# Degrees from run ends, divided loads, layer norm first, and rows of two groups gathered inside the block of degrees

## The chip, the cores and the metric

The kernel runs on one core of one Trainium2 chip. A core has TensorE (PE, matmuls into PSUM), VectorE (DVE), ScalarE (ACT), GpSimd (POOL, which also issues indirect DMAs) and SyncE (SP, which here only issues DMAs and waits), with 16 DMA engines. The metric is the device time of one execution in microseconds; lower is better.

## The reference

A graph of 12,500 nodes with 32 features and 200,000 edges, sorted by target (`dst`); each edge has 16 attributes. Two layers are computed:

```
h = relu(layernorm(x))
m = relu(concat(h[src], edge_attr) @ w1a + b1a) @ w1b + b1b      # per edge
agg = segment_sum(m, dst) / max(count of dst, 1)
x = x + relu(concat(h, agg) @ w2a + b2a) @ w2b + b2b
h = relu(layernorm(x)); f = h
10 times:  f = 0.9 * in_deg^-0.5 * segment_sum((f * out_deg^-0.5)[src], dst) + 0.1 * h
result = x + f
```

`in_deg` and `out_deg` are the numbers of edges that enter and leave a node, at least 1. Everything is float32.

## The kernel before, in words

Nodes stand as 128 partitions by J = 98 columns (node n at partition n mod 128, column n div 128). Edges stand as 128 partitions by T = 1568 columns, in the order of the input, so each partition holds a stretch of edges sorted by target; 704 padding edges fill the last partition. The work is a row of blocks. At the end of a block all engines wait for each other, SP's own waits on DMAs included. `fast_way` calls them in this order:

1. `setup`: SP loads x, the two ends of the edges and the weights, one DMA after another, and waits for all (`loaded`). Each of `src` and `dst` is one DMA of 127 partitions and one of the last, short row. SP then starts a DRAM-to-DRAM copy of all edge attributes (12.5 MB) and doesn't wait for it. VectorE waits for `loaded` and splits each end into partition and column.
2. `degrees(…, 1)`: in-degrees as a matrix product over all edges. For each of 98 groups of G = 16 edge columns, VectorE makes 16 one-hot rows of the partition (L298, 128x2048) and of the column (L298, 128x1568), and PE adds 16 products into one PSUM bank (L329).
3. `layer_norm_relu` on VectorE with one square root of ScalarE, then `store_table`: SP stores h to DRAM as the table of rows (L262) and waits for it.
4. `prepare_sorted`: VectorE works out, in single steps, marks of equal neighbours, keys of edges, and from the in-degrees the first and last edge of each node (L713 to L759). SP stores the keys.
5. `messages_and_counts`: a loop over 98 groups of 16 edge columns, two slots (s = 0, 1) in one pass of the loop. For a group GpSimd issues 16 indirect DMAs (L858), each of which gathers one row of the table for 128 edges, and one fetch of keys for two groups (L839); SP loads the group's attributes into the same rows tile (L884) and stores the counts (L871) and the running sums (L876). PE turns the rows (L1100), multiplies them with the weights (L1117), and counts pairs of source and target by one-hot products (L1083, L1089); ScalarE copies what PE turned (L1028), applies ReLU (L1032) and reads the counts (L1023); VectorE makes the one-hot rows (L963, L967) and adds the sums of runs (L928). GpSimd starts group g when PE has turned group g - 2, whose slot it takes, and VectorE has copied the indices of g (L939), which it does at the start of its own group g - 1.
6. `nodes_of_runs`, a second layer norm, `propagate` (the ten steps, from about 3,900 us on), `needs_general`, `store_result`.

`needs_general` makes a flag; if it isn't zero, `general_way` computes everything anew in a form that needs no sorted edges. It is not run on the reference's data.

Of the kernel before, what the change touches and what calls it, by code (L numbers as in the profile page):

```python
# [6 lines left out]
FP32 = mybir.dt.float32  # L7
BF16 = mybir.dt.bfloat16
FP16 = mybir.dt.float16
# [118 lines left out]

def setup(nc, b, edges, ins):

    with ExitStack() as ctx:
# [7 lines left out]
        LOADS = 17  # L139

        @block.sync
        def _(sp):
# [4 lines left out]
            for tile, ends in ((edges.src[:, 0:T], ins["src"]), (edges.dst, ins["dst"])):  # L147
                sp.dma_start(tile[0:P - 1, :], ends[0:(P - 1) * T].rearrange("(p t) -> p t", t=T)).then_inc(loaded, 16)
                sp.dma_start(tile[P - 1:P, 0:EL], ends[(P - 1) * T:E].rearrange("(p t) -> p t", p=1)).then_inc(loaded, 16)
# [116 lines left out]
def degrees(nc, b, edges, sides):  # L266
# [3 lines left out]
    with ExitStack() as ctx:  # L270
# [47 lines left out]
        def _(pe):  # L318
# [15 lines left out]
            last.then_inc(summed, 1)  # L334

# [314 lines left out]
def prepare_sorted(nc, b, edges, ins, kept):  # L650


    same, cont, last_row, window_row, unsorted = kept
    with ExitStack() as ctx:
# [49 lines left out]
        def _(dve):  # L704
# [20 lines left out]
            step(nc.vector.tensor_reduce(unsorted[:, 0:1], drop[:, :], AX.X, ALU.max))  # L725

# [20 lines left out]
            step(nc.vector.tensor_tensor(start[:, :], start[:, :], b.banks[:, 0, 0:J], ALU.add))  # L747
            nc.vector.tensor_copy(column[:, :], start[:, :]).then_inc(counted, 1)

            step(nc.vector.tensor_tensor(last[:, :], start[:, :], b.in_deg[:, :], ALU.add))  # L750
            step(nc.vector.tensor_scalar(last[:, :], last[:, :], -1.0, 0.0, ALU.add, ALU.max))
            step(nc.vector.tensor_scalar(part[:, :], last[:, :], 1.0 / T, 0.5 / T - 0.5, ALU.mult, ALU.add))
# [22 lines left out]
def messages_and_counts(nc, b, edges, same, window_row, tail, counted_edges, crowded):  # L775
# [8 lines left out]
    with ExitStack() as ctx:  # L784
        sem = lambda name: ctx.enter_context(nc.semaphore(f"{name}_{b.tag}"))
        sb = lambda name, shape, dt=FP32: ctx.enter_context(nc.sbuf_tensor(f"{name}_{b.tag}", shape, dt))
        gathered = [sem(f"gathered{s}") for s in range(SLOTS)]
# [13 lines left out]
        rows = sb("rows", [P, SLOTS, G, 64])  # L801
# [28 lines left out]
        def _(pool):  # L830
# [14 lines left out]
            with pool.Fori(0, n_loops) as i:  # L845
                for s in range(SLOTS):
# [10 lines left out]
                    for c in range(G):  # L857
                        pool.indirect_dma_start(out=rows[:, s, c, 0:DN], out_offset=None, in_=b.dram.table,  # L858
                                                in_offset=bass.IndirectOffsetOnAxis(ap=idx[:, s, c:c + 1], axis=0)) \
                            .then_inc(gathered[s], 16)  # L860
# [755 lines left out]
def fast_way(nc, ins, out, dram, flag):  # L1616

    with ExitStack() as ctx:
# [3 lines left out]
        unsorted = ctx.enter_context(nc.sbuf_tensor("unsorted", [P, 1], FP32))  # L1622
        with ExitStack() as edge_ctx:
# [5 lines left out]
            degrees(nc, b, edges, 1)  # L1629
            layer_norm_relu(nc, b, "in")  # L1630
            store_table(nc, b, b.h)
            prepare_sorted(nc, b, edges, ins, (same, cont, last_row, window_row, unsorted))
# [38 lines left out]
```

## Time and profile before

| | us |
|---|---|
| median of 3 runs (lowest to highest) | 8118.78 (8115.39 to 8119.13) |
| the profiled execution's own time | 8119.95 |
| its span in the profile | 8118.4 |
| busy in the span: PE, VectorE, ScalarE, GpSimd | 5850.0, 4429.2, 737.9, 1670.8 |

A row of the timeline gives start, duration, engine, line, operation, output and input tiles, and in brackets how long the engine had been idle and what released it; "SPq" is SP's queue issuing a DMA, and its time is that of the issue, not of the transfer. "issue" means that the engine waited for nothing that the profile shows, "remote" that the releaser is not among what it shows. A row of the stage table gives the stretch, then busy time (and instructions) of PE, PE's weight loads, VectorE, ScalarE and GpSimd, the granted TensorE clock, the DMA engines' share, and GB/s.

### The profile page before, as it was taken

To read this page: it belongs to the slowest core of one execution; us is meant where nothing else is said; L and a number is where in the kernel's file an instruction comes from. 1 tells how busy PE (TensorE), PEld (TensorE's weight loads), DVE (VectorE), ACT (ScalarE), POOL (GpSimd) and SP (SyncE) were. 2 spreads that over 40 slices of the span, in tenths; PEclk is the share of its full clock that TensorE was granted. 3 is DMA by queue.
4 is the path that set the end of the run, shared out by engine and by line. 5 is a ranking of instruction groups with operands and counts; after the bars stand their busy time and mean duration, and the time that the engine had idled before them with its cause. 6 is when DMAs were issued, how large, how long until landed. Compare 5 with 4: busy or idle time off the path is not lost. (4 is left out here: it accounts for less than half of the span.)

```text
span 8118.4 us, 215578 instructions
## 1 busy us (share of the span) xinstructions
PE 5850.0 (72%) x86684; PEld 3701.6 (46%) x86684; DVE 4429.2 (55%) x12772; ACT 737.9 (9%) x1743; POOL 1670.8 (21%) x1737
## 2 busy tenths in 40 slices
PE   5924444444444444443879999999999999999998
PEld 4723333333333333332435465556554655555555
DVE  4744444444444444443376666666666666666665
ACT  0012222222222222221100000000000000000000
POOL 0044444444444444445000000000000000000000
PEclk9986666666666666666589999999999999999999
DMA  2022222222222222221045555555555555555554
GB/s 80 0 66 60 60 60 64 60 60 61 62 60 60 60 60 60 63 60 51 4 180 193 201 191 199 193 201 191 200 193 201 192 201 193 193 197 198 202 193 173
DMA packets 442509, 1013.57 MB, mean 125 GB/s; under 512 B 253086, under 2 KB 371838, under 8 KB 387262
## 3 DMA queue, kind: packets, MB, share of 16 engines
q1 hardware_dynamic: 386878, 968.76, 33.6%
q0 software_dynamic: 54912, 33.89, 2.3%
q8 instruction: 614, 10.06, 0.5%
q14 instruction: 105, 0.86, 0.0%
HBM read 838.71 MB, written 176.58 MB: 125 GB/s over the span
## 5 line engine op out<-in xcount | busy, mean ns | idle before, releaser
L1529 PE MATMUL banks_fast<-count_units_fast,feature_parts_fast 128*32 128x512 fp8e3 x70608 | 3823.6, 379 | 50.3 <-DVE count_units_fast L1424 46.4
L1529 PEld LDWEIGHTS banks_fast<-count_units_fast,feature_parts_fast 128*32 128x32 bf16 x70608 | 2048.6, 97 | 1801.9 <-issue 54.1
L1423 DVE TENSOR_SCALAR count_units_fast<-packed_ring_fast 128x512 int32<-128x512 int32 x2949 | 1257.8, 427 | 1424.1 <-PE banks_fast L1529 1391.4
L858 POOL DMA_INDIRECT rows_fast<-row_table,idx_fast x1568 | 1508.8, 962 | 968.1 <-DVE idx_fast L939 489.8
L1117 PE MATMUL banks_fast<-w1a_b1a_fast,turn_fast 49*128 49x96 f32 x3136 | 372.5, 374 | 1815.5 <-ACT turn_fast L1028 1589.2
L1424 DVE TENSOR_SCALAR count_units_fast<-packed_ring_fast 128x512 int32<-128x512 int32 x2949 | 1240.3, 421 | 0.0
L1117 PEld LDWEIGHTS banks_fast<-w1a_b1a_fast,turn_fast 49*128 49x128 f32 x3136 | 293.3, 259 | 1913.7 <-ACT turn_fast L1028 1499.6
L963 DVE TENSOR_TENSOR window_src_hot_fast<-iota_by_windows_fast,window_keys_fast 128x1024 bf16<-128x1024 bf16 x392 | 270.3, 690 | 1585.5 <-PE banks_fast L1089 920.7
L967 DVE TENSOR_SCALAR window_place_hot_fast<-iota_wide_fast,local_keys_fast,target_weight_fast 128x196 bf16<-128x196 f16 x3136 | 929.7, 335 | 0.0
L1083 PE MATMUL banks_fast<-window_place_hot_fast,window_src_hot_fast 128*128 128x196 bf16 x3136 | 685.9, 310 | 43.9 <-issue 21.2
L1089 PE MATMUL banks_fast<-window_place_hot_fast,window_src_hot_fast 128*128 128x196 bf16 x3136 | 662.6, 303 | 0.0
L1023 ACT CAST count_stage_fast<-banks_fast 128x392 uint16<-128x392 f32 x784 | 396.3, 506 | 1701.9 <-remote 1139.2
L928 DVE SCALAR_TENSOR_TENSOR run_sums_fast<-run_sums_fast,same_target 128x96 f32<-128x96 f32 x1485 | 462.7, 312 | 37.7 <-DVE run_sums_fast L928 27.3
L1083 PEld LDWEIGHTS banks_fast<-window_place_hot_fast,window_src_hot_fast 128*128 128x128 bf16 x3136 | 404.6, 155 | 129.0 <-issue 60.4
L1089 PEld LDWEIGHTS banks_fast<-window_place_hot_fast,window_src_hot_fast 128*128 128x128 bf16 x3136 | 434.5, 154 | 0.0
L1399 ACT COPY drained_fast<-banks_fast 128x512 f32<-128x512 f32 x60 | 35.2, 587 | 3849.8 <-PE banks_fast L1529 3849.8
L329 PE MATMUL banks_fast<-place_hot_fast,part_hot_fast 128*128 128x98 bf16 x1568 | 289.0, 365 | 5.3 <-DVE place_hot_fast L298 5.3
L329 PEld LDWEIGHTS banks_fast<-place_hot_fast,part_hot_fast 128*128 128x128 bf16 x1568 | 229.8, 147 | 64.3 <-DVE place_hot_fast L298 5.4
L1032 ACT ACTIVATE run_sums_fast<-banks_fast 128x384 f32<-128x384 f32 x392 | 194.4, 496 | 560.3 <-remote 442.4
L1100 PE MATMUL banks_fast<-identity_fast,rows_fast 128*128 128x128 f32 x784 | 195.2, 340 | 21.4 <-DMA rows_fast<-row_table,idx_fast 21.4
L839 POOL DMA_INDIRECT raw_keys_fast<-edge_keys,key_idx_fast x50 | 45.9, 918 | 727.1 <-PE banks_fast L1100 717.1
L1028 ACT COPY turn_fast<-banks_fast 128x256 f32<-128x256 f32 x392 | 148.7, 379 | 332.2 <-remote 252.2
(241 smaller groups left out, 1934.2 us busy)
## 6 DMA issues: line engine op xcount, KB each, us to landing
packed_ring_fast<-edge_counts SPq DMA_DIRECT2D x422, 1792.0 KB, 7.2
edge_counts<-count_stage_fast SPq DMA_DIRECT2D x100, 784.0 KB
running_sums<-run_sums_fast SPq DMA_DIRECT2D x100, 768.0 KB
rows_fast<-row_table,idx_fast POOLq DMA_INDIRECT x1568
rows_fast<-attrs_padded SPq DMA_DIRECT2D x98, 128.0 KB
attrs_padded<-in_edge_attr SPq DMA_DIRECT2D x1, 12500.0 KB, 41.2
row_table<-h_nodes_fast SPq DMA_DIRECT2D x1, 1568.0 KB, 5.2
edge_keys<-keys_fast SPq DMA_DIRECT2D x1, 1568.0 KB, 5.1
```

Source lines behind the costliest of these rows:

```text
L329: last = nc.tensor.matmul(count[:, k, 0:J], part_hot[:, s, k, :, c], place_hot[:, s, k, :, c], start=False, stop=False, skip_group_check=True)
L858: pool.indirect_dma_start(out=rows[:, s, c, 0:DN], out_offset=None, in_=b.dram.table, in_offset=bass.IndirectOffsetOnAxis(ap=idx[:, s, c:c ...
L928: nc.vector.scalar_tensor_tensor(out=sums[:, s, c, :], in0=before, scalar=same[:, at], in1=sums[:, s, c, :], op0=ALU.mult, op1=ALU.add).th ...
L963: nc.vector.tensor_tensor(part_hot[:, q % 2, :, :], iota_by_windows[:, :, :], keys[:, s * WG + q * QW:s * WG + (q + 1) * QW].unsqueeze(1). ...
L967: nc.vector.tensor_scalar(place_hot[:, q % 2, w, :], iota_w[:, :], local[:, k:k + 1], weight[:, k:k + 1], ALU.is_equal, ALU.mult).then_inc ...
L1023: nc.scalar.copy(to, of).then_inc(count_read, 1)
L1083: last = nc.tensor.matmul(b.banks[:, C_BANK[u % 4], side * WC:(side + 1) * WC], part_hot[:, m, :, w], place_hot[:, m, w, :], start=(half = ...
L1089: last = nc.tensor.matmul(b.banks[:, S_BANK, half * WC:(half + 1) * WC], part_hot[:, m, :, w], place_hot[:, m, w, :], start=False, stop=Fa ...
L1117: last = nc.tensor.matmul(b.banks[:, M_BANK + k % 2, k // 2 * DH:(k // 2 + 1) * DH], turn[at:at + DI + 1, q % 2, (k // 2) * P:(k // 2 + 1) ...
L1423: nc.vector.tensor_scalar(to[..., 0:P // 8], of, NIBBLES, None, ALU.bitwise_and)
L1424: return nc.vector.tensor_scalar(to[..., P // 8:P // 4], of, 4, NIBBLES, ALU.logical_shift_right, ALU.bitwise_and)
L1529: last = nc.tensor.matmul(b.banks[at:at + DN, SWEEP[m % 2], 0:COLS], parts[:, side, j, k * DN:(k + 1) * DN], of_strip.bitcast(FP8), start= ...
```

## The change

- The loads of `src` and `dst` are divided: 112 partitions and 15 partitions, instead of 127 at once.
- Layer norm and the store of the table come right after `setup`. `degrees(…, 1)` is replaced by `sorted_degrees`, after them.
- `sorted_degrees` finds the last edge of each run of equal targets. Each partition is cut into 4 pieces of 392 edges; a key for each run end holds the node (relative to the partition's first) and the position. Four rounds of `max` (the 8 largest) and `match_replace` pull up to 32 keys out of each piece; what is left shows up in `overfull`, which is added to the flag. The difference of neighbouring positions is the number of edges in the run. These 128 keys in a partition are then added up like the edges before: 8 groups of 16, with one-hot rows of the partition, and of the column times the number of edges.
- In the same block GpSimd issues the gathers of the edge loop's groups 0 and 1 into the rows tile, which is now made by `fast_way` (class `Rows`). In the edge loop GpSimd fetches the keys of the first two passes ahead and starts with group 2.
- `prepare_sorted` gets two steps for the flag and two that keep starts and ends in range.

```
@@ setup
-        LOADS = 17
+        LOADS, EVEN = 19, 112
...
-                sp.dma_start(tile[0:P - 1, :], ends[0:(P - 1) * T].rearrange("(p t) -> p t", t=T)).then_inc(loaded, 16)
+                for lo, hi in ((0, EVEN), (EVEN, P - 1)):
+                    sp.dma_start(tile[lo:hi, :], ends[lo * T:hi * T].rearrange("(p t) -> p t", t=T)).then_inc(loaded, 16)

@@ class Rows
+    def gather(self, pool, b, s, idx):
+
+        for c in range(G):
+            pool.indirect_dma_start(out=self.rows[:, s, c, 0:DN], out_offset=None, in_=b.dram.table,
+                                    in_offset=bass.IndirectOffsetOnAxis(ap=idx[:, c:c + 1], axis=0)).then_inc(self.gathered[s], 16)

@@ sorted_degrees
+    PIECES, ROUNDS, TOP = 4, 4, 8
+    W, KEPT = T // PIECES, ROUNDS * TOP
+    LIST, SPAN = PIECES * KEPT, 512
...
+        @block.gpsimd
+        def _(pool):
+            nc.gpsimd.iota(position[:, :].rearrange("p (c w) -> p c w", c=PIECES), pattern=[[0, PIECES], [1, W]], base=1,
+                           channel_multiplier=0).then_inc(counted_off, 1)
+            for s in range(SLOTS):
+                ahead.gather(pool, b, s, edges.src[:, s * G:(s + 1) * G])
...
+            first = node[:, 0:1]
+            step(nc.vector.tensor_copy(iota_wide[:, :, :], b.iota16[:, :].unsqueeze(2).broadcast_to([P, P, G])))
+            step(nc.vector.scalar_tensor_tensor(out=node[:, :], in0=edges.dst_place[:, :], scalar=float(P),
+                                                in1=edges.dst_part[:, :], op0=ALU.mult, op1=ALU.add))
+            step(nc.vector.tensor_tensor(ends[:, 0:T - 1], node[:, 1:T], node[:, 0:T - 1], ALU.not_equal))
+            step(nc.vector.memset(ends[:, :].rearrange("p (c w) -> p c w", c=PIECES)[:, :, W - 1:W], 1.0))
+            step(nc.vector.tensor_scalar(key[:, :], node[:, :], first, float(SPAN), ALU.subtract, ALU.mult))
+            dve.wait_ge(counted_off, 1)
+            step(nc.vector.tensor_tensor(key[:, :], key[:, :], position[:, :], ALU.add))
+            step(nc.vector.tensor_tensor(key[:, :], key[:, :], ends[:, :], ALU.mult))
+            for r in range(ROUNDS):
+                for c in range(PIECES):
...
+                    nc.vector.max(out=best, in_=piece).then_inc(topped, 1)
+                for c in range(PIECES):
...
+                    nc.vector.match_replace(out=piece, in_to_replace=best, in_values=piece, imm_value=0.0).then_inc(replaced, 1)
+            dve.wait_ge(replaced, ROUNDS * PIECES)
+            step(nc.vector.tensor_reduce(overfull[:, :], key[:, :], AX.X, ALU.max))
...
+            for g in range(LIST // G):
+                s, of = g % 2, slice(g * G, (g + 1) * G)
+                dve.wait_ge(used, g + 1)
+                nc.vector.tensor_tensor(part_hot[:, s, :, :], iota_wide[:, :, :], part16[:, of].unsqueeze(1).broadcast_to([P, P, G]),
+                                        ALU.is_equal).then_inc(hot, 1)
+                nc.vector.tensor_tensor(place_hot[:, s, :, :], iota_wide[:, 0:J, :], place16[:, of].unsqueeze(1).broadcast_to([P, J, G]),
+                                        ALU.is_equal).then_inc(hot, 1)
+                dve.wait_ge(hot, 3 * g + 2)
+                nc.vector.tensor_tensor(edge_hot[:, s, :, :], place_hot[:, s, :, :], edges16[:, of].unsqueeze(1).broadcast_to([P, J, G]),
+                                        ALU.mult).then_inc(hot, 1)

@@ prepare_sorted
+            step(nc.vector.tensor_scalar(overfull[:, :], overfull[:, :], 0.0, None, ALU.is_gt))
+            step(nc.vector.tensor_tensor(unsorted[:, :], unsorted[:, :], overfull[:, :], ALU.max))
...
+            step(nc.vector.tensor_scalar(start[:, :], start[:, :], 0.0, float(E), ALU.max, ALU.min))
...
+            step(nc.vector.tensor_scalar(last[:, :], last[:, :], float(EP - 1), None, ALU.min))

@@ messages_and_counts, GpSimd
             fetch_keys(0)
-            with pool.Fori(0, n_loops) as i:
+            pool.wait_ge(keys_turned, 1)
+            pool.sem_inc(taken, 1)
+            fetch_keys(1)
+            with pool.Fori(1, n_loops) as i:

@@ fast_way
             setup(nc, b, edges, ins)
-            degrees(nc, b, edges, 1)
             layer_norm_relu(nc, b, "in")
             store_table(nc, b, b.h)
-            prepare_sorted(nc, b, edges, ins, (same, cont, last_row, window_row, unsorted))
-            messages_and_counts(nc, b, edges, same, window_row, tail, counted_edges, crowded)
+            ahead = Rows(nc, edge_ctx, "fast")
+            sorted_degrees(nc, b, edges, overfull, ahead)
+            prepare_sorted(nc, b, edges, ins, (same, cont, last_row, window_row, unsorted, overfull))
+            messages_and_counts(nc, b, edges, same, window_row, tail, counted_edges, crowded, ahead)
```

## Rows read from the trace of the kernel before

**Rows 1.** Stage table: degrees, layer norm, preparation, edge loop from its third group.

```profile
94.30:392.90 298.60, 289.32 (x1570) 230.03 (x1570) 212.66 (x208) 1.57 (x2) 0.00 (x0) 1.00 0.11 35
392.90:415.40 22.50, 0.00 (x0) 0.00 (x0) 21.09 (x13) 0.29 (x1) 0.00 (x0) 1.00 0.00 0
...
421.00:450.80 29.80, 1.83 (x8) 1.43 (x8) 26.00 (x34) 0.00 (x0) 3.15 (x8) 1.00 0.13 54
...
520.30:3701.20 3180.90, 1332.63 (x10129) 1145.01 (x10127) 1435.20 (x5500) 655.29 (x1575) 1522.10 (x1584) 0.65 0.22 61
```

**Rows 2.** Timeline, SP's issues in `setup`: x, then first and last small load.

```profile
9.53 10.07 SPq L146 DMA_DIRECT2D x_nodes_fast<-in_x  x1
...
63.29 0.89 SPq L151 DMA_DIRECT2D w1a_b1a_fast<-in_L_gnn_w1a  x1
...
72.86 0.28 SPq L159 DMA_DIRECT2D w2b_b2b_fast<-in_L_gnn_b2b  x1
```

**Rows 3.** DMA view of 21 to 84 us: what all DMA engines moved.

```profile
DMA packets 795, 1.70 MB, mean 27 GB/s; under 512 B 540, under 2 KB 540, under 8 KB 795
```

**Rows 4.** Timeline after the loads: VectorE's first split, SP's attribute copy.

```profile
84.97 0.98 DVE L189 TENSOR_SCALAR end_low_fast<-src_ends_fast 128x1568 int32<-128x1568 int32 x1 [76.29 <-DMA w2b_b2b_fast<-in_L_gnn_b2b]
...
86.84 0.60 SPq L165 DMA_DIRECT2D attrs_padded<-in_edge_attr  x1
```

**Rows 5.** DMA issues by line: size and us from issue to landing.

```profile
attrs_padded<-in_edge_attr SPq DMA_DIRECT2D x1, 12500.0 KB, 41.2
row_table<-h_nodes_fast SPq DMA_DIRECT2D x1, 1568.0 KB, 5.2
```

**Rows 6.** Groups by line and shape, 0 to 400 us: busy, mean ns, idle before.

```profile
L329 PE MATMUL banks_fast<-place_hot_fast,part_hot_fast 128*128 128x98 bf16 x1568 | 289.0, 365 | 5.3 <-DVE place_hot_fast L298 5.3
...
L298 DVE TENSOR_TENSOR part_hot_fast<-iota_by_columns_fast,part_fast 128x2048 bf16<-128x2048 bf16 x98 | 120.1, 1226 | 81.1 <-PE banks_fast L329 80.7 <-DVE place_fast L290 0.4
L298 DVE TENSOR_TENSOR place_hot_fast<-iota_by_columns_fast,place_fast 128x1568 bf16<-128x1568 bf16 x98 | 94.9, 969 | 0.0
```

**Rows 7.** Timeline, single VectorE passes: 3136, 1568 and 98 wide.

```profile
396.73 3.43 DVE L236 TENSOR_TENSOR h_nodes_fast<-x_nodes_fast,ln_mean_in_fast 128x3136 f32<-128x3136 f32 x1
...
421.18 1.79 DVE L714 SCALAR_TENSOR_TENSOR dst_number_fast<-dst_place_fast,dst_part_fast 128x1568 f32<-128x1568 f32 x1
...
429.13 1.79 DVE L725 TENSOR_REDUCE unsorted<-drop_any_fast 128x1 f32<-128x1568 f32 x1
...
446.78 0.21 DVE L751 TENSOR_SCALAR node_last_fast<-node_last_fast 128x98 f32<-128x98 f32 x1
```

**Rows 8.** Timeline, head of the edge loop up to group 2's gather.

```profile
463.95 0.43 SPq L884 DMA_DIRECT2D rows_fast<-attrs_padded  x1
464.60 0.97 POOL L858 DMA_INDIRECT rows_fast<-row_table,idx_fast  x1 [2.51 <-PEq L1069]
...
486.12 0.68 PE L1100 MATMUL banks_fast<-identity_fast,rows_fast 128*128 128x128 f32 x2 [21.36 <-DMA rows_fast<-row_table,idx_fast]
...
504.89 0.95 POOL L858 DMA_INDIRECT rows_fast<-row_table,idx_fast  x1 [0.30 <-issue]
...
510.46 0.37 ACT L1028 COPY turn_fast<-banks_fast 128x256 f32<-128x256 f32 x1 [5.73 <-remote]
...
520.29 0.95 POOL L858 DMA_INDIRECT rows_fast<-row_table,idx_fast  x1 [14.45 <-DVE idx_fast L939]
```

**Rows 9.** Line L1170, gathers of another stage: shortest, median and longest ns.

```profile
L1170 POOL DMA_INDIRECT run_last_rows_fast<-running_sums,run_last_idx_fast x98: 943/947/4111, 3741.8 to 3871.6; - x98
```

**Rows 10.** Timeline, middle of the edge loop, round the end of a gather.

```profile
1038.23 0.95 POOL L858 DMA_INDIRECT rows_fast<-row_table,idx_fast  x1 [0.30 <-issue]
...
1042.33 0.69 DVE L963 TENSOR_TENSOR window_src_hot_fast<-iota_by_windows_fast,window_keys_fast 128x1024 bf16<-128x1024 bf16 x1 [13.99 <-remote]
1042.38 0.50 ACT L1023 CAST count_stage_fast<-banks_fast 128x392 uint16<-128x392 f32 x1 [17.49 <-remote]
...
1049.48 0.95 POOL L858 DMA_INDIRECT rows_fast<-row_table,idx_fast  x1 [10.30 <-DVE idx_fast L939]
```

More of the change, by code:

```diff
@@ L126, in __init__ @@
         self.dst_place = sb("dst_place", [P, T])
+class Rows:
+    def __init__(self, nc, ctx, tag):
+        self.rows = ctx.enter_context(nc.sbuf_tensor(f"rows_{tag}", [P, SLOTS, G, 64], FP32))
+        self.gathered = [ctx.enter_context(nc.semaphore(f"gathered{s}_{tag}")) for s in range(SLOTS)]
+    def gather(self, pool, b, s, idx):
+        for c in range(G):
+            pool.indirect_dma_start(out=self.rows[:, s, c, 0:DN], out_offset=None, in_=b.dram.table,
+                                    in_offset=bass.IndirectOffsetOnAxis(ap=idx[:, c:c + 1], axis=0)).then_inc(self.gathered[s], 16)
 def setup(nc, b, edges, ins):
@@ L650, in prepare_sorted @@
 def prepare_sorted(nc, b, edges, ins, kept):
-    same, cont, last_row, window_row, unsorted = kept
+    same, cont, last_row, window_row, unsorted, overfull = kept
     with ExitStack() as ctx:
@@ L772, in _, with messages_and_counts @@
             last.then_inc(summed, 1)
-def messages_and_counts(nc, b, edges, same, window_row, tail, counted_edges, crowded):
+def messages_and_counts(nc, b, edges, same, window_row, tail, counted_edges, crowded, ahead):
     Q = 4
@@ L786, in messages_and_counts @@
         sb = lambda name, shape, dt=FP32: ctx.enter_context(nc.sbuf_tensor(f"{name}_{b.tag}", shape, dt))
-        gathered = [sem(f"gathered{s}") for s in range(SLOTS)]
+        rows, gathered = ahead.rows, ahead.gathered
         attrs_in = [sem(f"attrs_in{s}") for s in range(SLOTS)]
@@ L800, in messages_and_counts @@
         idx = sb("idx", [P, SLOTS, G], I32)
-        rows = sb("rows", [P, SLOTS, G, 64])
         turn = sb("turn", [P, 2, 2 * P])
@@ L856, in _ @@
                     pool.sem_inc(taken, 1)
[L857 to L860, printed above, removed]
+                    ahead.gather(pool, b, s, idx[:, s, :])
         @block.sync
@@ L1622, in fast_way @@
         unsorted = ctx.enter_context(nc.sbuf_tensor("unsorted", [P, 1], FP32))
+        overfull = ctx.enter_context(nc.sbuf_tensor("overfull", [P, 1], FP32))
         with ExitStack() as edge_ctx:
```

69 lines of the change are left out of this document (added).

## The prediction

> **What bounds the kernel now.** I read the stage table first, then the timeline of the loads, the groups of the degrees block, and the waits of the edge loop. The reader sees in the stage table [rows 1] that the span is a line of stages one after the other. The change touches the start and the head of the edge loop: 84.9 us of loads, 76.3 of them without any engine's work [rows 4]; 298.6 us of degrees, in which PE is busy for 289.3; 22.5 us of layer norm plus the table's store (on to 421.0); 29.8 us of preparation; and the edge loop, 3180.9 us from its third group on. All are in series, so what a stage loses the span loses, unless something hidden under it comes to light.
>
> **Loads (setup).** SP issues x first and the issue of its short second part ends at 19.6 [rows 2]. Between 21 and 84 us the DMA engines move 1.70 MB, at 27 GB/s [rows 3]: the two loads of 127 partitions. The last issue is at 72.86, yet VectorE starts only at 84.97 [rows 2, 4]: the small loads stand behind the second big one. The change cuts each into 112 and 15 partitions. Rows that bound the new speed: the table's store, 1.6 MB over 128 partitions, lands in 5.2 us [rows 5]; at 27 GB/s nothing is gained. I take the store's row for the 112. The 15 partitions are 94 KB each, 3.5 us each at 27 GB/s if nothing changes for them, under 1 us otherwise. Sum: x done at 19.6; six issues of about 0.4 (2.4) and 4 us of data partly under them, to about 24.5; the eleven small loads took 63.29 to 73.14, 9.85 us, which now nothing hides, to 34.5; landing 1.5: 36. **Gain 49 us**; bounds 42 (everything in series, 15 partitions slow) and 57 (the small issues at 0.4 each, some having waited for the queue). "DMA: Bandwidth & Descriptors", section "Why a DMA increments its semaphore by 16 and not by 1", of the Trainium skill says that the DMA takes the largest number of engines up to 16 that divides the slowest dimension, so one for 127, 16 for 112 and 15 for 15; by it the 15 partitions cost under 1 us, which would make the gain about 51 instead of 49.
>
> **Layer norm and table first.** The 22.5 us of layer norm are the same work [rows 1]. But the copy of the edge attributes, issued 2.0 us after the loads land (86.84) and 41.2 us long, now lies under it instead of under the degrees [rows 4, 5]. The splits take 9.4 us and layer norm 22.5, so the table's store is issued 32.4 us after the loads, while the copy runs until 43.2; both go out on SP's queue. The small loads behind the long one [rows 2, 4] say that what is issued later on it waits. So the store lands at about 43.2 + 4 = 47.2 instead of 37.6. From the end of the splits to the start of the next block: 38.3 us instead of 28.1, **loss 10 us**. Bounds: 0 (the queue shares) and 13. All engines stand at the block's end until SP has it; nothing else fills that time.
>
> **Degrees.** Removed: 98 groups of 16 matmuls, 289.0 us [rows 6], and 9.6 us around them, of which the last 3.5 (in_deg, reciprocals, root) stay. Added on VectorE, before any matmul: a 2048-wide copy 1.23 [rows 6], four two-input passes of 1568 at 1.79, a one-input pass at 0.98 [rows 4], a tiny memset, and gaps of 0.03 [rows 7]: 9.6 us. Then 16 max and 16 match_replace of 392 elements. The trace has neither; the nearest row is the reduction of 1568 at 1.79 [rows 7], and a 98-wide pass is 0.21, which puts 392 at 0.5 to 0.57: 32 x 0.55 = 17.6, the round's four pieces hiding each other's waits. Bounds: 12, and 35 if each makes two passes. One reduction 1.8, twelve passes of 128 at 0.25: 3.0. So 32.0 us to the first group. Then eight groups of one-hots, 1.23 + 0.97 + 0.97 by busy time, 3.1 in pace, against 2.95 for PE's 16 matmuls [rows 6]: VectorE sets the pace, 24.8. Last group of PE 2.95, tail 3.5: 63.3 us.
>
> Beside it GpSimd makes its iota (about 2) and 32 gathers at 1.25 [rows 8]: 42 us, under the 63. The edge loop's rows show one price of that: with the last gather ending at 1039.2, ScalarE and VectorE, which both wait for PE's signals, go on at 1042.3, after 17.5 and 14.0 us of idleness, though the matmuls that they wait for stand 15 us earlier [rows 10]; VectorE's waits for itself go on at pace meanwhile. I take that as: while GpSimd issues gathers, PE's signals reach the others late. In the new block VectorE's group 2 waits for PE's first group at 38.2 us; held until 42 + 3.1 that is 6.8 more: **70 us against 298.6, gain 228**. Bounds 56 (fast max, no hold) and 95 (slow max, hold, gaps). A stall of this kind can't be dearer than 45 us from the block's start, since the gathers end.
>
> A rule speaks against this part. With GpSimd in its gathers beside VectorE at work, the loop's gathers keep a pitch of 1.25 us [rows 8, 10]; but the max, the replacing and the float passes of 1568 stand in no row beside a gather. "SBUF — State Buffer", section "SBUF: two separate sides", of the Trainium skill says that a VectorE instruction in a two-port mode locks GpSimd out, so that it cannot write its DMAs' descriptors, about 3.1 us instead of 0.6 in its example; it is what the Trainium skill has behind rival C.
>
> **Preparation.** Two [128,1] steps at about 0.2 and two of 98 at 0.24 are added in VectorE's chain of single steps: **+0.9 us**.
>
> **Edge loop.** The old loop gathers group 0 at 464.60, then group 1; PE begins at 486.12, when the first 16 have landed, ScalarE and PE go on at 510.46 after the second 16 (last one issued 504.89, ending 505.8), and the gather of group 2 starts at 520.29, 55.7 us after the first [rows 8]. From there each group is one gather (20.3) and 12 to 13 us of work after it: GpSimd idles 10.30 before the next [rows 10]. The gather of a group thus lies in series, though it has two buffers. In the new loop groups 0 and 1 are in place. PE then waits for the attribute rows only, issued at 463.95 [rows 8], about 3 us; the ReLU waits for the first store of sums and the first counts for the store of counts, both issued within 2.5 us of 463.95 behind each other (1.6 MB, 4 to 6 us): about 472.5. With no gather in flight, ScalarE's second turn comes at about 473 instead of 510.46, and the rest, 9.8 us, to the third gather is the same: 483 instead of 520.3. **Gain 37 us**; bounds 19 (only PE's earlier start, 467 for 486) and 40. From the third gather on nothing differs.
>
> **Sum**, against the profiled execution's own 8120.0 us (span 8118.4): 8120.0 - 49 + 10 - 228 + 0.9 - 37 = 7816.9. That execution is 1.2 above the median of 8118.78, so I forecast 7816 us.
>
> **Rivals.**
> A. The loop's head gains only PE's start. For it: the stores of counts and sums stand before ScalarE's first work, and a wait of PE on ScalarE has several causes; against: ScalarE still stood 5.7 us before 510.46 [rows 8], 44 us after those stores went out. 37 becomes 19: 7834.
> B. SP's queue doesn't hold the table's store behind the copy, and PE's signals aren't held in the block. For it: the copy and the store are different in kind; against: [rows 2, 4, 10]. 10 and 7 us back: 7800. The Trainium skill, in "DMA: Bandwidth & Descriptors", section "Queues, rings and completion order", says that each DMA engine takes a queue's descriptors in order, which speaks for the loss of 10.
> C. VectorE's long passes slow GpSimd's gathers, and the block ends with them. The dearest regular case at hand: a gather of 128 rows in another stage, median 0.947 but up to 4.1 us [rows 9]. At 3.9 for all 32: 125 us, block 130 instead of 70: 7877. It decides above 2.1 us a gather (32 x 2.1 = 67). Against: the pitch of 1.25 beside VectorE at work.
> D. The other side, slower than before: more than 32 runs end in one piece of 392 edges. Then `overfull` raises the flag and the whole general way runs after the fast one. Its loop has 1568 columns in each of 13 passes, each with a 128x3136 pass of VectorE, 3.43 us for such a size [rows 7]: 70 ms, some 78,000 us in all. At 16 edges a node a piece ends 25 runs on average, so it takes 33 or more; in the reference's own data the fullest of the 512 pieces has 31. Almost excluded.
>
> **How the numbers follow.** The forecast 0.68, A 0.13, B 0.09, C 0.06, D 0.01, and 0.03 for costs that I don't see. Own range: 7795 to 7845 (loads -8/+7, top-k -6/+17, store -10/+3). With A and B in it and part of the way to C: 7782 to 7862. About 0.2% (16 us) is what a measurement of this kernel can tell from no change; a loss of 290 us somewhere would be needed to get there, which only D, or a mistake of kind, gives: faster 0.97, same 0.01, slower 0.02.
>
> **What would show it.** VectorE's first split near 36 us; the table's store landing near 83; the new block near 70 us, with its max near 0.5 us each, and VectorE standing at its third group until 3 us after the last gather; the gather of group 2 some 18 us after the loop's first attribute load, and then 66.5 us for two groups, as before. Wrong would be: max above 1 us each, gathers longer than 1.3 us in pitch, VectorE not standing in the block (the signals' hold is then no matter of gathers), or PE waiting in group 0 of the loop until a store lands.

## The result

The changed kernel takes **7805.9 us** (median of 4 runs, 7805.0 to 7808.3), the kernel before 8118.6 in the same comparison (8115.4 to 8119.1): ratio 0.9616, 95% interval 0.9599 to 0.9633. The forecast was 7816, the range 7782 to 7862. The profiled execution's span went from 8118.4 to 7803.3, 315.1 us less; the terms of the forecast come to 303.1.

All experiments below are timed against the kernel before on their own chip. On two of the chips the kernel before takes about 6863 us instead of 8118, and there the edge loop runs in another rhythm (experiment 7). I call the chips of 8118 us the first kind and those of 6863 us the second.

### The profile page after: what moved, and what is told of

Same layout as the page of the kernel before. It is cut to its first block and busy times, and to the rows that moved or that the text cites. A ratio compares the mean times of both kernels' runs of the same rounds, so it can differ in the third digit from the quotient of the medians.

```text
span 7803.3 us, 211998 instructions
## 1 busy us (share of the span) xinstructions
PE 5569.6 (71%) x85242; PEld 3465.7 (44%) x85242; DVE 4278.7 (55%) x12669; ACT 737.2 (9%) x1743; POOL 1673.8 (21%) x1738
## 5 line engine op out<-in xcount | busy, mean ns | idle before, releaser
L139 POOL DMA_INDIRECT rows_fast<-row_table,idx_fast x1536 | 1475.9, 961 | 958.4 <-DVE idx_fast L1075 491.9
L1236 PEld LDWEIGHTS banks_fast<-identity_fast,rows_fast 128*128 128x128 f32 x784 | 116.6, 178 | 2.2 <-DMA rows_fast<-attrs_padded 2.2
L1306 POOL DMA_INDIRECT run_last_rows_fast<-running_sums,run_last_idx_fast x98 | 100.6, 1027 | 70.8 <-DVE run_last_idx_fast L1311 41.3
## 6 DMA issues: line engine op xcount, KB each, us to landing
row_table<-h_nodes_fast SPq DMA_DIRECT2D x1, 1568.0 KB, 15.3
```

The costliest lines, as they stand in the source:

```text
L139: pool.indirect_dma_start(out=self.rows[:, s, c, 0:DN], out_offset=None, in_=b.dram.table, in_offset=bass.IndirectOffsetOnAxis(ap=idx[:, c ...
L1236: last = nc.tensor.transpose(b.banks[:, T_BANK, k * P:(k + 1) * P], rows[:, s, c:c + 2, :].rearrange("p c d -> p (c d)"), b.ident[:, :])
```

## The profile after, beside that of before

The stage table of the changed kernel (columns as in [rows 1]): layer norm, the block of degrees, the preparation, and the edge loop from group 2's gather on, over the same 96 groups.

```profile
40.60:62.90 22.30, 0.00 (x0) 0.00 (x0) 21.09 (x13) 1.53 (x2) 0.00 (x0) 1.00 1.02 325
78.70:151.80 73.10, 24.88 (x128) 18.26 (x128) 59.25 (x101) 0.29 (x1) 39.02 (x34) 1.00 0.04 8
151.80:181.90 30.10, 1.84 (x8) 1.43 (x8) 26.73 (x38) 0.00 (x0) 3.11 (x8) 1.00 0.13 54
212.60:3388.40 3175.80, 1315.63 (x10130) 1129.93 (x10128) 1439.74 (x5501) 654.67 (x1575) 1519.26 (x1584) 0.66 0.23 61
```

The block of 298.60 us has become one of 73.10, in which VectorE (59.25) and not PE (24.88) is the busiest. Layer norm and preparation are as they were, and the loop is the old one less 5 us.

Where the 315 us come from, from the same boundaries in both timelines (first split, start of layer norm, start and end of the block, start of the loop's block, group 2's gather, first gather of `nodes_of_runs`, span):

| term | before | after | difference | forecast |
|---|---|---|---|---|
| loads, to the first split | 84.97 | 30.68 | -54.3 | -49 |
| layer norm and store | 28.06 | 38.14 | +10.1 | +10 |
| block of degrees | 298.15 | 73.05 | -225.1 | -228 |
| preparation | 29.95 | 30.35 | +0.4 | +0.9 |
| loop's block to group 2's gather | 69.25 | 30.51 | -38.7 | -37 |
| from there to the end | 7598.1 | 7590.7 | -7.5 | 0 |

**Loads.** The timeline of the changed kernel: SP's issues, and VectorE's first split, which the last small load releases.

```profile
9.54 10.10 SPq L160 DMA_DIRECT2D x_nodes_fast<-in_x  x1
19.68 0.79 SPq L163 DMA_DIRECT2D src_ends_fast<-in_src  x2
...
21.64 0.25 SPq L164 DMA_DIRECT2D dst_ends_fast<-in_dst  x1
21.93 0.32 SPq L166 DMA_DIRECT2D w1a_b1a_fast<-in_L_gnn_w1a  x1
...
25.70 0.28 SPq L174 DMA_DIRECT2D w2b_b2b_fast<-in_L_gnn_b2b  x1
...
30.68 0.98 DVE L204 TENSOR_SCALAR end_low_fast<-src_ends_fast 128x1568 int32<-128x1568 int32 x1 [22.01 <-DMA w2b_b2b_fast<-in_L_gnn_b2b]
```

The eleven small issues go out between 21.93 and 25.98 (4.1 us) where they took 9.85 [rows 2]. The transfers of 127 partitions had held up the issues too, the small ones and above all those of the short last rows. In the kernel before, the timeline has for these rows:

```profile
19.92 13.11 SPq L149 DMA_DIRECT2D src_ends_fast<-in_src  x1
33.55 29.69 SPq L149 DMA_DIRECT2D dst_ends_fast<-in_dst  x1
```

In the changed kernel the same issues take 0.25 us each.

**Store of the table.** The changed kernel's page, DMA issues, with size and us from issue to landing:

```profile
attrs_padded<-in_edge_attr SPq DMA_DIRECT2D x1, 12500.0 KB, 42.0
row_table<-h_nodes_fast SPq DMA_DIRECT2D x1, 1568.0 KB, 15.3
```

The store lands 15.3 us after its issue instead of 5.2 [rows 5]: 10.1 us more, in which no engine works, and all of the +10.1.

**Degrees.** The changed kernel's timeline, VectorE: one round of max and replace, then the first products of the one-hots with their buffers' waits.

```profile
89.78 1.97 DVE L413 MAX8 sorted_top_fast<-sorted_key_fast 128x8 f32<-128x392 f32 x4
91.67 0.07 DVE L417 MATCH_VALUE_LOAD sorted_key_fast<-sorted_top_fast,sorted_key_fast 128x8 f32 x1
91.72 0.55 DVE L417 MATCH_REPLACE8 sorted_key_fast<-sorted_top_fast,sorted_key_fast 128x392 f32<-128x392 f32 x1
...
111.51 1.23 DVE L437 TENSOR_TENSOR sorted_part_hot_fast<-ted_iota_by_columns_fast,sorted_part_fast 128x2048 f16<-128x2048 f16 x1
...
123.34 1.23 DVE L437 TENSOR_TENSOR sorted_part_hot_fast<-ted_iota_by_columns_fast,sorted_part_fast 128x2048 f16<-128x2048 f16 x1 [5.68 <-remote]
...
129.03 1.23 DVE L437 TENSOR_TENSOR sorted_part_hot_fast<-ted_iota_by_columns_fast,sorted_part_fast 128x2048 f16<-128x2048 f16 x1 [2.57 <-remote]
...
135.41 1.23 DVE L437 TENSOR_TENSOR sorted_part_hot_fast<-ted_iota_by_columns_fast,sorted_part_fast 128x2048 f16<-128x2048 f16 x1 [0.23 <-PE banks_fast L463]
```

And PE with GpSimd in the same stretch of the changed kernel:

```profile
80.33 1.88 POOL L139 DMA_INDIRECT rows_fast<-row_table,src_ends_fast  x1 [0.17 <-issue]
82.52 1.37 POOL L139 DMA_INDIRECT rows_fast<-row_table,src_ends_fast  x1 [0.30 <-issue]
84.19 2.03 POOL L139 DMA_INDIRECT rows_fast<-row_table,src_ends_fast  x1 [0.30 <-issue]
...
95.87 0.95 POOL L139 DMA_INDIRECT rows_fast<-row_table,src_ends_fast  x1 [0.30 <-issue]
...
114.68 6.21 PE L463 MATMUL banks_fast<-sorted_edge_hot_fast,sorted_part_hot_fast 128*128 128x98 f16 x32 [114.68 <-DVE sorted_edge_hot_fast L442]
...
125.69 1.59 POOL L139 DMA_INDIRECT rows_fast<-row_table,src_ends_fast  x1 [0.30 <-issue]
```

PE ends its first 32 products at 120.9 (the first 16 of them at about 117.8), and VectorE's third group, which needs only the first 16, starts at 123.34; its fourth, which needs the second 16, at 129.03, 1.7 us after the last gather (127.3). After that the waits are 0.2. The hold is 8.25 us long in all (5.68 and 2.57); the forecast had 6.8. It isn't quite the hold that the forecast described: VectorE goes on at 123.34 while the gathers run to 127.3, and stands a second time. PE's signals come 5.5 and 8.1 us after the ends of their products, and not all at once after the last gather. (The starts of matmuls are read from the trace, their ends are modelled. So the rows don't tell a late signal from a late end of the last matmul; "late signal" stands for both here.)

**Loop head.** The changed kernel's timeline; what stood between 464.60 and 520.29 [rows 8]:

```profile
194.82 0.43 SPq L1020 DMA_DIRECT2D rows_fast<-attrs_padded  x1
...
197.61 0.69 PE L1236 MATMUL banks_fast<-identity_fast,rows_fast 128*128 128x128 f32 x2 [1.99 <-DMA rows_fast<-attrs_padded]
...
202.57 0.49 ACT L1168 ACTIVATE run_sums_fast<-banks_fast 128x384 f32<-128x384 f32 x1 [3.86 <-DMA running_sums<-run_sums_fast]
203.32 0.39 ACT L1164 COPY turn_fast<-banks_fast 128x256 f32<-128x256 f32 x1
...
212.65 0.96 POOL L139 DMA_INDIRECT rows_fast<-row_table,idx_fast  x1 [14.85 <-DVE idx_fast L1075]
```

PE waits for the attribute rows (1.99), the ReLU for the store of sums (3.86), and group 2's gather comes 17.8 us after the attribute load. In the middle of the loop the gap before a gather is 10.3 us, as before.

## Experiments

**1. The divided loads alone.** The kernel before with this edit:

```
-        LOADS = 17
+        LOADS, EVEN = 19, 112
...
-                sp.dma_start(tile[0:P - 1, :], ends[0:(P - 1) * T].rearrange(...)).then_inc(loaded, 16)
+                for lo, hi in ((0, EVEN), (EVEN, P - 1)):
+                    sp.dma_start(tile[lo:hi, :], ends[lo * T:hi * T].rearrange(...)).then_inc(loaded, 16)
```

> The kernel before with the loads of src and dst divided into 112 and 15 partitions, and nothing else. Theory (the loads are in series and everything after them keeps its length): VectorE's first split moves from 84.97 to 30.7 us as in the changed kernel, time 8118.6 - 54.3 = 8064. Rival (part of the loads' gain comes back later, because the attribute copy now starts earlier beside other work): more than 8068.

Measured: 8064.4 us against 8117.6, ratio 0.9935 (0.9920 to 0.9951). 53.2 us by the medians, against 54.3 between the first splits: the loads' gain stands alone, and nothing later takes back more than about a microsecond of it. (The interval of the ratio is 12 us wide to either side; the medians and the timelines agree much more closely.)

**2. Layer norm and store ahead of the old degrees.** On top of 1:

```
-            degrees(nc, b, edges, 1)
             layer_norm_relu(...)
             store_table(nc, b, b.h)
+            degrees(nc, b, edges, 1)
```

> The kernel before with divided loads, and with layer norm and the table's store ahead of the old degrees block. Theory (SP's queue holds the table's store behind the attribute copy): 10.6 us more than with divided loads alone, 8075; the store's issue-to-landing time about 15 us. Rival (the order is free, the 10 us of the changed kernel come from something new in it): 8064.

Measured: 8071.7 us against 8117.6, ratio 0.9945 (0.9930 to 0.9960), 7.2 more than experiment 1. By the timelines the preparation starts 10.0 us later (376.75 for 366.78), and the loop happens to be 2.7 us shorter. Its page has for the two DMAs:

```profile
attrs_padded<-in_edge_attr SPq DMA_DIRECT2D x1, 12500.0 KB, 41.8
row_table<-h_nodes_fast SPq DMA_DIRECT2D x1, 1568.0 KB, 15.1
```

The order alone costs the 10 us of the timeline, and the store's landing (15.1) holds them; against the span, the loop's 2.7 hide a part. Rival B's half about the queue has fallen.

**3. No gathers ahead.** The changed kernel, with the edge loop starting at group 0 and its own gathers:

```
-            for s in range(SLOTS):
-                ahead.gather(pool, b, s, edges.src[:, s * G:(s + 1) * G])
...
-            pool.wait_ge(keys_turned, 1)
-            pool.sem_inc(taken, 1)
-            fetch_keys(1)
-            with pool.Fori(1, n_loops) as i:
+            with pool.Fori(0, n_loops) as i:
```

> The changed kernel without the gathers ahead: GpSimd only makes its iota in the block of degrees, and the edge loop gathers all groups as before. Theory (PE's signals are late while GpSimd gathers): in the block of degrees VectorE no longer stands at its third and fourth group, the block takes 73.1 - 8.2 = 65 us, and the head of the loop is 69.3 us again instead of 30.5: 7806 - 8 + 38.7 = 7837. Rival 1 (VectorE stands there for PE's own pace): the block stays at 73, 7845. Rival 2 (the loop's head gains only PE's earlier start): 7806 - 8 + 19 = 7817.

Measured: 7833.1 us, ratio 0.9653 (0.9640 to 0.9667), against 0.9616. The block shrinks from 73.1 to 64.5 us and the stretch from the loop's block to `nodes_of_runs` grows from 3246.8 to 3284.2. So the gathers ahead cost 8.6 in the block and bring 37.4 up to `nodes_of_runs`, 28.8 net; by the medians, which come from two comparisons, it is 27.2 (7833.1 for 7805.9). VectorE's waits in this kernel's block:

```profile
116.73 1.23 DVE L435 TENSOR_TENSOR sorted_part_hot_fast<-ted_iota_by_columns_fast,sorted_part_fast 128x2048 f16<-128x2048 f16 x1 [0.22 <-PE banks_fast L461]
...
123.11 1.23 DVE L435 TENSOR_TENSOR sorted_part_hot_fast<-ted_iota_by_columns_fast,sorted_part_fast 128x2048 f16<-128x2048 f16 x1 [0.21 <-PE banks_fast L461]
```

Without gathers the third group waits 0.22 us instead of 5.68: the hold belongs to the gathers.

**4. GpSimd busy with iotas instead.** Experiment 3 with 32 iotas of 128x1568 on GpSimd in the block:

```
+            for k in range(32):
+                nc.gpsimd.iota(busy[:, :], pattern=[[1, T]], base=k, channel_multiplier=0).then_inc(idled, 1)
+                pool.wait_ge(idled, k + 1)
```

> As the kernel without gathers ahead, but GpSimd runs 32 iotas of 128x1568 (about 1.5 us each, 48 us) in the block of degrees, where the changed kernel gathers. Theory H1 (PE's signals are late whenever GpSimd is busy): VectorE stands some 5 to 8 us at its third group again, block 71 to 73 us. Theory H2 (it is the gathers, their descriptors or their DMAs, that hold the signals): no standing, block 65 us, as without the gathers ahead, about 7837 in all.

Measured: 7849.9 us, ratio 0.9673 (0.9658 to 0.9687); block 77.7 us. It does not decide what it was made for: the iotas end at 129.4, before VectorE first needs a signal of PE in that kernel (its third group, at 130.2, waits 0.23). The 13 us are another effect, in this kernel's timeline:

```profile
79.67 49.74 POOL L387 IOTA sorted_busy_fast<- 128x1568 int32 x32
...
108.47 1.47 DVE L423 TENSOR_SCALAR sorted_end_int_fast<-sorted_top_int_fast 128x128 int32<-128x128 int32 x1
109.98 1.47 DVE L424 TENSOR_SCALAR sorted_local_int_fast<-sorted_top_int_fast 128x128 int32<-128x128 int32 x1
```

The same passes take 0.23 us beside gathers. Ten passes in a row of this size and with one input take 1.47 here, which is about the length of one iota (1.55), and together they make up nearly all of the 13 us. The two-input passes, the reduction (1.79), max and replace keep their times. I read it as a pass that waits out the iota that is running. The Trainium skill, "SBUF — State Buffer", section "Who interferes with whom", has a VectorE pass in a two-port mode and GpSimd shut each other out for the whole instruction. The 1.47 agrees with that, if these passes run in such a mode, which no row shows.

**5. The attribute copy after the store.** The changed kernel with

```
-            setup(nc, b, edges, ins)
+            setup(nc, b, edges, ins, late=True)        # without the copy of the attributes
...
-            store_table(nc, b, b.h)
+            store_table(nc, b, b.h, ins["edge_attr_16"])   # store, wait for it, then issue the copy
```

> The changed kernel with SP starting the attribute copy after the table's store has landed, not before. Theory (the store waits behind the copy on SP's queue): the store lands in about 5 us and the block of degrees starts 10.6 us earlier; the copy (42 us) lies under that block (73 us): 7806 - 10.6 = 7795. Rival (the copy beside the gathers slows them or the block): block longer than 75 us, no gain.

> The changed kernel with the attribute copy started after the table's store, again, now beside the changed kernel on the same chip. Theory: 9.5 us less than it (the store lands in 5 us instead of 15). Rival: the copy beside the gathers costs the loop or the block what the store gains, 0.

Both runs fell on chips of the second kind. Measured in the first comparison 6551.4 us, ratio 0.9545 (0.9532 to 0.9558), the kernel before being 6863.5. In the second, beside the changed kernel itself: 6550.4, ratio 0.9546 (0.9533 to 0.9559), against 6564.5, ratio 0.9564 (0.9551 to 0.9577). The intervals touch, so what decides is the page, which has the store at 5.2 us again, and the timelines: the block starts at 69.18 instead of 79.14, and the span is 10.2 us shorter (6548.7, 6558.9).

```profile
attrs_padded<-in_edge_attr SPq DMA_DIRECT2D x1, 12500.0 KB, 42.3
row_table<-h_nodes_fast SPq DMA_DIRECT2D x1, 1568.0 KB, 5.2
```

This is the best whole kernel measured, ahead of both, on the chips where it ran.

**6. Four buffers for the one-hots.** The changed kernel with

```
-        part_hot, place_hot = sb("part_hot", [P, 2, P, G], FP16), sb("place_hot", [P, 2, J, G], FP16)
-        edge_hot = sb("edge_hot", [P, 2, J, G], FP16)
+        part_hot, place_hot = sb("part_hot", [P, 4, P, G], FP16), sb("place_hot", [P, 4, J, G], FP16)
+        edge_hot = sb("edge_hot", [P, 4, J, G], FP16)
```

> The changed kernel with four buffers for the one-hot rows in the block of degrees instead of two, so that VectorE waits for PE's signal of group g - 4 instead of g - 2. Theory (PE's signals arrive 5 to 8 us late while GpSimd gathers, all else is ready): VectorE's stands at the third and fourth group go, the block takes 65 to 67 us, 7798. Rival (PE itself is late, its matmuls not only its signals): PE sets the pace from its first group, the block stays above 71 us, 7806.

> The changed kernel with four buffers for the one-hot rows, again. Where PE's signals are late: VectorE waits for groups g - 4, whose signals have come by then; block 65 to 67 us instead of 73, 7798. Rival (the signals come as late, or the last one does): block above 71. Where they aren't late: no difference, block 64 to 65, 6562.

Measured: 6562.5, ratio 0.9561 (0.9548 to 0.9574), and in the second comparison 6559.3, ratio 0.9557 (0.9544 to 0.9570), where the changed kernel has 0.9564: no difference clear of noise. Nor could there be much of one, since on these chips the changed kernel has no hold to take away (7). The block is 64.0 us long with four buffers and 65.0 with two. With experiment 5 in one kernel:

> The changed kernel with both: the attribute copy after the table's store, and four buffers. Theory: the gains add, 10.6 + 8: 7787. Rival (they take the same slack, or the copy delays the gathers so that they end the block): 7795 or more.

6554.4, ratio 0.9552 (0.9539 to 0.9565), level with experiment 5.

**7. The changed kernel itself on the second kind of chip.**

> The changed kernel itself, once more, beside the two that follow on one chip, since the last four runs came from a chip on which the kernel before takes 6863 us instead of 8118 and PE's signals weren't late. Where the kernel before takes about 8118: 7806, the block of degrees 73 us with VectorE standing 5 to 8 us. Where it takes about 6863: the block 65 us, no gain at the loop's head beyond PE's earlier start and the two gathers that leave GpSimd's queue (20 to 40 us), 6562 in all. Rival for that chip: the gain is smaller than 290, as the gathers there were hidden anyway.

Measured: 6564.5 us against 6862.7, ratio 0.9564 (0.9551 to 0.9577): 298 us, against 313 on the first kind. Its block takes 65.0 us. The timeline: VectorE's third group in the block, and in the loop PE, GpSimd and ScalarE.

```profile
118.22 1.23 DVE L437 TENSOR_TENSOR sorted_part_hot_fast<-ted_iota_by_columns_fast,sorted_part_fast 128x2048 f16<-128x2048 f16 x1 [0.20 <-PE banks_fast L463]
...
1007.95 0.69 PE L1236 MATMUL banks_fast<-identity_fast,rows_fast 128*128 128x128 f32 x2 [8.01 <-DMA rows_fast<-row_table,idx_fast]
1009.25 0.94 POOL L139 DMA_INDIRECT rows_fast<-row_table,idx_fast  x1 [0.30 <-issue]
1010.41 0.49 ACT L1168 ACTIVATE run_sums_fast<-banks_fast 128x384 f32<-128x384 f32 x1 [1.37 <-PE banks_fast L1253]
...
1029.39 0.69 PE L1236 MATMUL banks_fast<-identity_fast,rows_fast 128*128 128x128 f32 x2 [7.81 <-DMA rows_fast<-row_table,idx_fast]
```

The same instructions as in the changed kernel's first trace, gathers beside them, and nobody waits long for PE's signals: ScalarE's ReLU goes on 1.37 us after its last work, in the middle of the gathers. There a group takes 21 us, which is 16 gathers at 1.3, and PE waits 7 to 8 us a group for rows. The first trace, at the same place:

```profile
1007.07 0.69 PE L1253 MATMUL banks_fast<-w1a_b1a_fast,turn_fast 49*128 49x96 f32 x8 [1.75 <-issue]
...
1016.59 0.49 ACT L1168 ACTIVATE run_sums_fast<-banks_fast 128x384 f32<-128x384 f32 x1 [9.65 <-remote]
...
1026.63 0.49 ACT L1159 CAST count_stage_fast<-banks_fast 128x392 uint16<-128x392 f32 x1 [9.54 <-remote]
```

The ReLU that needs the matmuls of 1007.07 starts at 1016.59. A group takes 33.2 us.

The stage `nodes_of_runs` shows the same thing apart from the edge loop. GpSimd there issues 98 gathers at a pitch of 1.25 us, while PE, ScalarE and VectorE pass pieces of work to each other. The first trace (its last gather ends at 3559.1), two steps beside gathers and one after them:

```profile
3502.81 0.47 ACT L1382 ACTIVATE run_mid_fast<-banks_fast,b2a_col_fast 48x256 f32<-48x256 f32 x1 [19.76 <-remote]
3514.01 0.22 DVE L1358 TENSOR_TENSOR x_nodes_fast<-x_nodes_fast,banks_fast 128x64 f32<-128x64 f32 x1 [20.89 <-remote]
...
3611.69 0.22 DVE L1358 TENSOR_TENSOR x_nodes_fast<-x_nodes_fast,banks_fast 128x64 f32<-128x64 f32 x1 [2.22 <-PE banks_fast L1421]
```

and the trace on the second kind, beside gathers:

```profile
2323.19 0.22 DVE L1358 TENSOR_TENSOR x_nodes_fast<-x_nodes_fast,banks_fast 128x64 f32<-128x64 f32 x1 [2.21 <-PE banks_fast L1421]
```

With the gathers over, the first chip has the second chip's waits (2.22 and 2.21 us). The two spans of the changed kernel differ by 1244 us: 8 lie in the block, about 1163 in the edge loop and 73 in `nodes_of_runs`. The whole difference between the two kinds is thus in stages in which GpSimd gathers.

**8. Half of the gathers.** The changed kernel with 8 of a group's 16 gathers, everywhere:

```
-    def gather(self, pool, b, s, idx):
+    def gather(self, pool, b, s, idx, columns=G):
...
-                    pe.wait_ge(gathered[s], (i + 1) * (G * 16))
+                    pe.wait_ge(gathered[s], (i + 1) * (G // 2 * 16))
```

> The changed kernel with only 8 of the 16 gathers of every group; it leaves out half of the rows, whose messages are then made of what stands in the tile. Theory (a group of the edge loop is one gather and some 13 us of work in series, since PE's signals are late while GpSimd gathers): each of the 96 groups gets 8 x 1.25 = 10 us shorter, two groups take 46.5 us instead of 66.5, about 6850 in all. Rival (the gathers have two buffers and 12 us of slack a group, something else sets 33 us a group): below 20 us gained, about 7800.

Measured: 6007.7 us, ratio 0.8754 (0.8741 to 0.8768), on the second kind of chip: two groups take 31 us there instead of 42.5. The expectation's numbers were for the first kind. Hence the last run, with the halving in the loop alone and four buffers, which fell on the first kind (8119.0 before):

```
-                    ahead.gather(pool, b, s, idx[:, s, :])
+                    ahead.gather(pool, b, s, idx[:, s, :], G // 2)
...
-                    pe.wait_ge(gathered[s], (i + 1) * (G * 16))
+                    pe.wait_ge(gathered[s], i * (G // 2 * 16) + G * 16)
```

> The changed kernel with four buffers for the rows gathered ahead, and with half of the gathers left out in the edge loop alone (8 of 16 a group; the 32 in the block of degrees all stand). It leaves out half of the rows of the loop's groups, so its time says nothing of a whole kernel. Theory (where the kernel before takes about 8118 us, TensorE's signals come late because GpSimd issues indirect DMAs, 33.2 us for a group of 16 gathers): half the gathers a group make two groups 46.5 us instead of 66.4, the time about 6850 us; and with four buffers the block of degrees stays at 70 to 73 us, since the signals still come late, unless a buffer was what VectorE waited for, in which case it is 65 to 67. Rival (the loop's group is bound by something else than its gathers): two groups shorten by less than 10 us, the time above 7400 us. Where the kernel before takes about 6863 us: block 64 us, two groups 31 us, about 6000 us as in the earlier run with half the gathers.

Measured: 6740.0 us, ratio 0.8300 (0.8286 to 0.8313). Two groups take 44.3 us (46.5 expected; 48 x 2.2 = 106 us are nearly the difference between 6850 and 6740). The block takes 63.9 us. This kernel's timeline, in the loop:

```profile
1008.38 0.69 PE L1253 MATMUL banks_fast<-w1a_b1a_fast,turn_fast 49*128 49x96 f32 x8 [3.22 <-issue]
...
1011.70 0.94 POOL L139 DMA_INDIRECT rows_fast<-row_table,idx_fast  x1 [0.30 <-issue]
...
1014.38 0.49 ACT L1168 ACTIVATE run_sums_fast<-banks_fast 128x384 f32<-128x384 f32 x1 [6.12 <-remote]
```

and its stage table, block and loop:

```profile
78.70:142.60 63.90, 24.38 (x128) 18.23 (x128) 58.85 (x100) 0.29 (x1) 43.34 (x34) 1.00 0.06 9
204.40:2320.00 2115.60, 1316.51 (x10106) 1133.01 (x10104) 1436.59 (x5490) 648.28 (x1574) 782.75 (x813) 0.75 0.31 85
```

Taking 16 gathers out of two groups takes 22.1 us out, a bit more than the 20 of the gathers themselves: on the first kind of chip a gather is fully in series in the loop, as the forecast read it from [rows 10]. ScalarE's wait ends 1.7 us after the last gather (1012.64), so the signals are late here as well, and still the block has no stall. VectorE's fifth group comes 5.9 us after the end of PE's first 16 products, and finds the signal there; with two buffers it needed it at 117.7. The first release in the changed kernel came 5.5 us after PE's end and fits. The second came 8.1 us after and would have cost 2.3 here (the sixth group starts 5.8 after), which didn't show. So four buffers remove the hold; how late a signal comes isn't one number. Of the 9.2 us between the two blocks, 8.25 are the hold; about 1 us four buffers bring on the second kind too (6). The block of the changed kernel with four buffers and the late copy together was not run on this kind of chip; by the two parts it would gain 9 and 10 us (an estimate).

## Why the prediction was right

Term by term the forecast is off by -5 (loads), 0 (store), +3 (block), -0.5 (preparation), -2 (loop's head) and -7.5 (rest), together -12 us on the profiled execution. The terms and their causes were right; two readings inside them were not, and are named below.

- **Loads, -54.3 for -49.** The step was right, and the mis-sized term is "the eleven small loads took 9.85 us, which now nothing hides": they took 4.1. They also began 2.6 us earlier (21.93 for 24.5) and landed 4.7 us after the last issue instead of 1.5. The bound at which "the small issues" had "waited for the queue" (57) was nearer. Before, from 21 to 84 us, the core's 16 DMA engines were busy for 7.0% of their time, which is about one engine; in the changed kernel, from 20 to 31 us, for 73.4%, at 163 GB/s. The rule on the number of engines, one for 127 partitions and 16 for 112, agrees with these shares (its estimate was 51 us): the Trainium skill, "DMA: Bandwidth & Descriptors", section "Why a DMA increments its semaphore by 16 and not by 1".
- **Store behind the copy, +10.1 for +10.** Experiment 2 has it alone, and experiment 5 takes it away. The copy, issued at 32.57, ends at 74.6, the store lands at 78.3, 3.7 later. The Trainium skill, "DMA: Bandwidth & Descriptors", section "Queues, rings and completion order", has each DMA engine take a queue's descriptors in order, which agrees.
- **Block, -225.1 for -228.** VectorE's first one-hot came 32.8 us after the block's start (32.0 forecast), by errors that nearly cancel: the 2048-wide copy changes type from bf16 to fp16 and took 2.50 instead of 1.23, the small passes took 3.7 instead of 3.0, and the four rounds took 16.2 instead of 17.6 (max 0.50, replace 0.56). The hold was 8.25 for 6.8, and here luck helped. The forecast held VectorE's third group until 3.1 us after the last gather, and had the gathers end at 42 us of the block. They ended at 48.6, so its own rule would have held the group until 51.7, some 12.8 us. It went on at 44.6, with gathers still to come, and the fourth group at 50.3, beyond the 45 us that the prediction had as the latest. So the step "held until" the gathers end failed: what the rows show is a signal that comes 5.5 to 8.1 us late. That this belongs to the gathers is shown (experiment 3, and `nodes_of_runs` in 7); that any work of GpSimd would do it was not shown, since experiment 4 missed the moment. Nor is it shown what in a gather does it. It holds for the chip of the forecast; on the second kind the block has none (65.0 us).
- **Gathers beside float passes.** They were in no row before: they took 1.37 to 2.22 us beside the first passes of the block, 0.95 beside max and replace and while VectorE stood, and 1.36 to 1.72 beside the one-hot passes (1568 and 2048 wide). Their mean pitch was 1.46 us, so one of the prediction's signs of being wrong ("gathers longer than 1.3 us in pitch") was there: the 42 us for the gathers were too few by 6.6. Rival C decided only above 2.1 us a gather for all 32; the sum here was 37.5 us busy, the end at 48.6 us from the block's start, under VectorE's 69.5. The mechanism behind C is thus there, with a slowing up to a factor of 2.3, but mostly beside two-input passes, and too small to end the block.
- **Loop head, -38.7 for -37**, and -37.4 by experiment 3: right, with the waits where they were forecast. Rival A has fallen.
- **Rest, -7.5, not forecast.** About 5 lie in the loop from group 2 on (3180.9 to 3175.8), over 96 groups whose code is unchanged. The same stretch of code moves by as much between kernels that don't differ in it: from the loop's block to `nodes_of_runs` 3290.7 us before, 3289.5 in experiment 1, 3286.7 in 2, 3284.2 in 3, 3284.0 in 4. What does it stays open.

The number was right also on a matter that it did not know: the hold and the 33-us groups are properties of the chip it was measured on. On the second kind the same change gives 298 us, 15 less, although the block is 8 us shorter there. If the old block of degrees takes the same time there (GpSimd is idle in it), the other terms bring some 23 us less, an estimate. The likely place is the loop's head, where the gathers are partly hidden anyway, but no trace of the kernel before was taken on that kind, so it isn't shown.

## What to carry over

A large load over 127 partitions, which ran at 27 GB/s here, is worth two DMAs, and it holds up the issues behind it as well as itself. When work is moved to an earlier place, look at what its DMAs now stand behind on their queue: here a store of 1.6 MB waited 10 us with all engines idle, and issuing the long copy second gave it back. Spare gathers under another engine's stage are worth more than the stall that they bring (37.4 for 8.6, on the first kind of chip), and two more buffers for the engine that stalls take that away too.

## What was not expected of the hardware

- **PE's signals during GpSimd's gathers are late on some chips only.** With the same kernel, ScalarE waits 9.65 us for PE in the loop on one chip and 1.37 on another; the kernel before takes 8118 and 6863 us. Gathers are as long in both (0.95, pitch 1.25). In `nodes_of_runs` VectorE waits 20.89 us beside gathers on the one and 2.21 on the other, and 2.2 on both once the gathers are over. What differs in the chips is open.
- **A 128x128 VectorE pass with one input beside an iota** of GpSimd took 1.47 us instead of 0.23; beside indirect DMAs 0.23 to 0.43.
- **Gathers beside VectorE** took 0.95 us beside max and replace, 1.4 to 2.2 beside two-input passes 1568 or 2048 wide.
